# A two-block convolution network on one core: a partition shuffle moved from TensorE to transfers

## The reference

```python
x = x + L0(_gn(x), p1, p3, p4, p5, p6)
x = x + L1(_gn(x), conv_w, gamma, beta)
```

```python
t1 = einsum('nchw,he->ncew', x, p1)                      # e = 16
t3 = depthwise conv of t1, 9 x 9, weights p3
t4 = grouped conv of t3, 5 x 1, four channels a group, p4
t5 = einsum('ncew,ewf->ncf', t4, p5)                     # f = 384
t6 = depthwise conv of t5 over f, 3 taps, p6
out = einsum('ncf,nfp->ncp', t6, t2) / sqrt(384)         # t2: three row shifts of x
```

## Time and profile before

| | |
|---|---|
| median of 3 runs | 300.83 us |
| lowest and highest | 298.19 and 301.51 us |
| the profiled execution's own time | 300.65 us |
| its span in the profile | 298.9 us |
| TensorE busy, share of the span | 85% |
| VectorE | 77% |
| ScalarE | 62% |
| GpSimd | 47% |

### The profile page before, as it was taken

How to read it: one execution, slowest core, us unless ns; L and a number is a source line. 1 busy time by engine, 2 the same in 40 slices (tenths; PEclk the granted TensorE clock), 3 DMA queues, 4 the chain that set the end, 5 groups by cost and what they waited for, 6 DMA issues and landing times.

```text
span 298.9 us, 6443 instructions
## 1 busy us (share of the span) xinstructions
PE 253.4 (85%) x2558; PEld 193.1 (65%) x2558; DVE 230.4 (77%) x543; ACT 186.6 (62%) x262; POOL 140.0 (47%) x136
## 2 busy tenths in 40 slices
PE   8999979989798998999999999999999999850000
PEld 4444456555454877988899889988899886630000
DVE  1898974454456777688999999999999997786991
ACT  2799613325344534776778877877778877456990
POOL 4000000005033204787988889888988889640000
PEclk9999979999999999999999999999999999975555
DMA  7996122432200700000000000000000000001798
GB/s 220 411 409 260 41 86 83 141 130 83 72 4 3 279 4 0 0 0 2 0 2 2 0 3 0 0 2 0 1 2 0 0 1 2 1 0 50 315 403 355
DMA packets 8445, 25.18 MB, mean 84 GB/s; under 512 B 1248, under 2 KB 1376, under 8 KB 8416
## 3 DMA queue, kind: packets, MB, share of 16 engines
q1 hardware_dynamic: 7184, 20.32, 18.7%
q10 hardware_dynamic: 1232, 4.46, 3.9%
HBM read 16.39 MB, written 8.39 MB: 83 GB/s over the span
## 4 chain that ended last, share of the span: by engine, by line
PE 75%; DVE 10%; issue 5%; DMA 2%; POOL 2%; ACT 2%; DVEq 0%; POOLq 0%; ACTq 0%
PE low L232 10%; PE low L234 9%; PE low L233 9%; PE low L562 9%; PE low L586 8%; DVE x_sb L986 5%; PE high L621 5%; PE high L699 4%; PE high L232 4%; PE high L234 4%; PE high L233 4%; PE high L708 3%; DMA x_sb<-in_x 2%; PE high L601 2%; DVE t_sb L778 2%
## 5 line engine op out<-in xcount | busy, mean ns | idle before, releaser
L379 POOL TENSOR_TENSOR g_lo<-y_sb,g_hi 128x1024 fp32r<-128x1024 f32 x15 | 36.1, 2408 | 14.4 <-ACT y_sb L521 14.4
L355 POOL TENSOR_TENSOR g_lo<-y_sb,g_hi 128x1024 fp32r<-128x1024 f32 x15 | 35.9, 2390 | 13.6 <-ACT g_hi L478 13.6
L232 PE MATMUL low<-g_hi,t_hi 128*128 128x512 f32 x96 | 37.6, 391 | 1.3 <-DVE t_lo L886 0.7
L234 PE MATMUL low<-g_hi,t_lo 128*128 128x512 f32 x96 | 37.5, 391 | 0.0
L233 PE MATMUL low<-g_lo,t_hi 128*128 128x512 f32 x96 | 37.5, 390 | 0.0
L346 POOL TENSOR_TENSOR p_lo<-p_raw,p_hi 128x384 fp32r<-128x384 f32 x4 | 3.9, 1004 | 65.2 <-ACT p_hi L443 65.2
L519 ACT ACTIVATE g_hi<-x_sb,rs 128x1024 fp32r<-128x1024 f32 x15 | 19.9, 1329 | 18.7 <-POOL rs L364 18.7
L562 PE MATMUL low<-xa,p_blk 128*128 128x512 f32 x64 | 28.0, 595 | 0.2 <-DVE xa L770 0.2
L770 DVE STREAM_TRANSPOSE xa<-x_sb 128x512 f32<-128x512 f32 x32 | 19.9, 681 | 8.5 <-DMA x_sb<-in_x 8.2
L857 DVE TENSOR_TENSOR x_sb<-x_sb,low 128x512 f32<-128x512 f32 x32 | 21.7, 677 | 6.1 <-PE low L234 5.9
L232 PE MATMUL high<-p_hi,d_split 128*128 128x384 f32 x68 | 24.5, 360 | 0.0
(11 more groups left out here) (156 smaller groups left out, 664.4 us busy)
## 6 DMA issues: line engine op xcount, KB each, us to landing
out<-x_sb SPq DMA_DIRECT2D x6, 1024.0 KB, 4.9
x_sb<-in_x SPq DMA_DIRECT2D x11, 512.0 KB, 9.4
x_sb<-in_x ACTq DMA_DIRECT2D x8, 512.0 KB, 13.8
taps<-in_taps SPq DMA_DIRECT2D x6, 320.0 KB, 3.7
mix<-in_mix SPq DMA_DIRECT2D x6, 256.0 KB, 3.2
out<-x_sb SPq DMA_DIRECT2D x3, 512.0 KB, 2.8
p_raw<-in_p SPq DMA_DIRECT2D x1, 768.0 KB, 5.8
taps_third<-in_taps SPq DMA_DIRECT2D x2, 320.0 KB, 4.5
```

The source lines that it names most:

```text
L232: nc.tensor.matmul(ps, w[0], m[0], start=start, stop=False)
L234: return nc.tensor.matmul(ps, w[1], m[0], start=False, stop=stop)
L355: pool.tensor_tensor(g1_lo[:, W:W + HW], y_sb[:, n, :], g1_hi[:, W:W + HW].bitcast(F32), ALU.subtract).then_inc(s["g1_lo"], 1)
L379: pool.tensor_tensor(g2_lo[:, :], y_sb[:, n, :], g2_hi[:, :].bitcast(F32), ALU.subtract).then_inc(s["g2_lo"], 1)
```

## The change

For the steps 0 to 4 (`RS = 5`) the permutation by identity products goes. In its place sixteen transfers from `t4_sb` to a new tensor `d_st` (three slots) carry the same blocks: six from SP, ten from GpSimd. The steps 5 to 7 keep the identity products. The conversions of d follow two steps behind instead of one (`D_AT`): steps 4 and 5 both stand behind the t3 copy of step 6. The mix product of steps 1 to 5 waits for the copy of t4 instead of the rest of d; the copy of t4 of step r waits until the transfers of step r - 2 have read the slot.

`d_st` takes the space of images 9 to 11, so seven images instead of four are loaded again, now also behind the output products of two images. Image two has buffers of its own for g1 in the space of images 14 and 15, and its conversion waits for no product. In turn 1 VectorE takes the first half of the moments ahead of the second addition. The load of w moves ahead of the last wait for a mix product.

The core of the diff:

```diff
-RESIDENT = 12
-TR = 3
+RESIDENT = 9
+USED_FIRST = 12
+RS = 5
+D_AT = {2: (0,), 3: (1,), 4: (2,), 5: (3,), 6: (4, 5), 7: (6,)}
+BY_SP = 6
+TR, DR = 3, 3
...
+        d_st = put("d_st", [DR, CI, B, JC * NO])
...
+        cursor[0] = region_t - 2 * HW * 4
+        second_hi = put("second_hi", [HW], F32R)
+        second_lo = put("second_lo", [HW], F32R)
...
+        def shuffle(eng, r, some, done):
+
+            eng.wait_ge(s["t4_ev"], 2 * (r + 1))
+            if r >= DR:
+                eng.wait_ge(s["d_lo"], 2 * (r - DR + 1))
+            for jl, co in some:
+                eng.dma_start(d_st[32 * jl:32 * jl + 32, r % DR, co].rearrange("p b k -> p (b k)"),
+                              t4_sb[32 * co:32 * co + 32, r % 2, jl].rearrange("p b k -> p (b k)")
+                              ).then_inc(done[r % DR], 16)
+
+        def shuffled(eng, r):
+            for done, some in ((d_in, BY_SP), (d_in_pool, len(blocks) - BY_SP)):
+                eng.wait_ge(done[r % DR], 16 * some * (r // DR + 1))
...
                 load_taps(r)
+                if r == R - 1:
+                    sp.dma_start(w_raw[:, :, :], w_in).then_inc(s["w_raw"], 16)
                 sp.wait_ge(s["d_mm"], 2 * (r - TR + 1))
                 load_mix(r)
+                shuffle(sp, r - TR, blocks[:BY_SP], d_in)
...
+            for r in range(RS):
+                shuffled(sp, r)
             sp.wait_ge(s["d_mm"], 2 * R)
-            sp.wait_ge(s["perm"], R)
+            sp.wait_ge(s["perm"], R - RS)
+            sp.wait_ge(s["o_mm"], 2)
...
+            for r in range(RS - 1):
+                shuffle(pool, r, blocks[BY_SP:], d_in_pool)
             for jc in range(JC):
                 pool.wait_ge(s["p5_hi"], jc + 1)
...
+            shuffle(pool, RS - 1, blocks[BY_SP:], d_in_pool)
             pool.wait_ge(s["gst"], 1)
...
             def d_high(r):
-                act.wait_ge(s["perm"], r + 1)
+                if r < RS:
+                    shuffled(act, r)
+                else:
+                    act.wait_ge(s["perm"], r - RS + 1)
...
-                if r >= 1:
-                    d_high(r - 1)
+                for q in D_AT.get(r, ()):
+                    d_high(q)
...
-                if n >= 1:
+                if n >= 2:
                     act.wait_ge(s["o_mm"], n)
-                act.copy(g1_hi[:, W:W + HW], g1_f(n)).then_inc(s["g1_hi"], 1)
+                (hi, _), first = g1_parts(n)
+                act.copy(hi[:, first:first + HW], g1_f(n)).then_inc(s["g1_hi"], 1)
...
-                    if t == MID and r >= 2:
+                    if t == MID and r - 2 >= RS:
                         permute(r - 2)
...
-                if 1 <= r < R - 1:
+                if 1 <= r <= RS:
+                    pe.wait_ge(s["t4_ev"], 2 * r)
+                elif RS < r < R - 1:
                     pe.wait_ge(s["d_lo"], 2 * r)
...
-                    if r >= 2:
-                        dve.wait_ge(s["perm"], r - 1)
+                    if r - 2 >= RS:
+                        dve.wait_ge(s["perm"], r - 2 - RS + 1)
+                    elif r >= 2 and h == 0:
+                        shuffled(dve, r - 2)
...
-                d_low(r)
+                for q in D_AT.get(r + 1, ()) if r < R - 1 else (R - 1,):
+                    d_low(q)
...
-                if t == N:
+                if t in (1, N):
                     x1_half(t - 1, 0)
```

More of the change, by code:

```diff
@@ L145, in build @@
         cursor[0] = region_t - (N - RESIDENT) * HW * 4
+        d_st = put("d_st", [DR, CI, B, JC * NO])
         t4_sb = put("t4_sb", [2, JL, B, JC * NO])
+        assert cursor[0] >= region_t - (N - USED_FIRST) * HW * 4
         taps_third = put("taps_third", [TCOLS])
         mix_third = put("mix_third", [MCOLS])
+        assert cursor[0] <= region_t
+        cursor[0] = region_t - 2 * HW * 4
+        second_hi = put("second_hi", [HW], F32R)
+        second_lo = put("second_lo", [HW], F32R)
         assert cursor[0] <= region_t
@@ L200, in build @@
         x_in = [sem(f"s_x_in{n}") for n in range(N)]
+        d_in = [sem(f"s_d_in{k}") for k in range(DR)]
+        d_in_pool = [sem(f"s_d_in_pool{k}") for k in range(DR)]
         taps_sem = [sem(f"s_taps_in{k}") for k in range(TR)]
@@ L220, in g2_parts, with g1_parts @@
             return (g2_hi, g2_lo) if n < N - 1 else (last_hi, last_lo)
+        def g1_parts(n):
+            return ((second_hi, second_lo), 0) if n == 1 else ((g1_hi, g1_lo), W)
         def g1_f(n):
@@ L252, in d_columns @@
         def d_columns(r, h):
+            if r < RS:
+                return d_st[:, r % DR, 2 * h:2 * h + 2, :, :].rearrange("p c b (j n) -> p b j n c", j=JC)
             return ps_mix(r)[:, 2 * h:2 * h + 2, :].rearrange("p c (b j n) -> p b j n c", b=B, j=JC)
+        blocks = [(jl, co) for jl in range(JL) for co in range(CI)]
+        def shuffle(eng, r, some, done):
[9 more added lines that the diff above has]
+                eng.wait_ge(done[r % DR], 16 * some * (r // DR + 1))
         block = ctx.enter_context(nc.Block())
@@ L288, in _ @@
                          allow_slow_non_contiguous=True).then_inc(s["p6_in"], 16)
-            sp.wait_ge(s["x_used"], 2 * (N - RESIDENT))
+            sp.wait_ge(s["x_used"], 2 * (N - USED_FIRST))
             sp.wait_ge(s["t1_mm"], NO)
@@ L354, in g1_low @@
                 pool.wait_ge(s["g1_hi"], n + 1)
-                pool.tensor_tensor(g1_lo[:, W:W + HW], y_sb[:, n, :], g1_hi[:, W:W + HW].bitcast(F32),
+                (hi, lo), first = g1_parts(n)
+                pool.tensor_tensor(lo[:, first:first + HW], y_sb[:, n, :], hi[:, first:first + HW].bitcast(F32),
                                    ALU.subtract).then_inc(s["g1_lo"], 1)
@@ L662, in out_product @@
                 pe.wait_ge(s["g1_lo"], n + 1)
+                (hi, low_part), first = g1_parts(n)
                 for hh in range(2):
@@ L667, in out_product @@
                         i0, i1 = (1 if hh == 0 and k == 0 else 0), H // 2 - (1 if hh and k == 2 else 0)
-                        lo, to = (H // 2 * hh + k) * W, HALF * hh
+                        lo, to = (H // 2 * hh + k - 1) * W + first, HALF * hh
                         mm = split_product(ps_o[:, to + W * i0:to + W * i1], (t6_hi[:, k, :], t6_lo[:, k, :]),
-                                           (g1_hi[:, lo + W * i0:lo + W * i1], g1_lo[:, lo + W * i0:lo + W * i1]),
+                                           (hi[:, lo + W * i0:lo + W * i1], low_part[:, lo + W * i0:lo + W * i1]),
                                            k == 1, k == 2)
@@ L787, in d_low @@
                     ins.then_inc(s["d_lo"], 1)
-            halves = [(n, hh) for n in (*range(RESIDENT, N), *range(BY_ACT, RESIDENT)) for hh in range(2)]
+            halves = [(n, hh) for n in (*range(USED_FIRST, N), *range(BY_ACT, USED_FIRST)) for hh in range(2)]
             for n, hh in halves:
@@ L948, in _ @@
                     x1_add(t - 1, 1)
-                    if t < N:
+                    if 1 < t < N:
                         x1_half(t - 1, 0)
```

1 line of the change is left out of this document (removed).

## The result

| | us |
|---|---|
| before, median of 22 runs beside the changed kernel | 299.31 (297.36 to 301.85) |
| changed kernel, median of 22 runs | 303.81 (299.60 to 309.24) |
| ratio | 1.0087 [1.0057, 1.0116] |
| changed kernel again, another set, 4 runs | 304.47 (302.58 to 307.13) |
| ratio there | 1.0160 [1.0112, 1.0208] |

A ratio leaves out the runs that lie over 1.5% above the fastest of the same kernel, nine of the changed kernel's 22 here. By the ratios the change costs 0.9% in the one set and 1.6% in the other, about the 1% that can be told from none and above it; by the medians of all runs it costs 1.5% and 2.0%. I had forecast 1.4% less. The first profiled execution of the changed kernel, 309.24 us (span 307.5), is the longest of its 22 runs, so a second was profiled in the other set: 304.03 us (span 302.3). What follows is read in both, and the second is the one to go by.

A forecast was written before the change was run, and what follows sets the result against it. The prediction took TensorE's own work and the handovers to it as the bound of the convolution stage; 3.0 us there plus 1.0 us at image two off 300.65 gave 296.65, stated as 296.6 us, range 294.0 to 318.0.

The forecast's parts named there:

- 4.45: Convolution stage: us gained on TensorE by removing five permutations, 0.89 per round, taken as the most possible.
- a = 0.47: GpSimd's issue pitch, us per transfer, taken from SP's image loads; bounds 0.26 and 2.2.
- The first rival: GpSimd's issue bounds the convolution stage at a pitch of 0.66 or more: 308 us at 0.8, 318.0 at 1.0; chance 0.30.
- Image two: Start of the long stage: image two's output products start at 116.1 instead of 117.14, gain 1.0 us (0.6 to 1.3).
- the formula behind step three's t4: Time from step three's share on GpSimd to step four's landing: twenty issues, p5 subtraction 3.88, completion 2.0 us; landing at 83.1.
- three and four come to 67.8 and 74.05: Ends of the t4 copies of steps three and four, in us, with three and four permutations gone before them; earlier 70.50 and 77.61.
- traffic alone isn't their cause, and I count them as unchanged: Convolution stage: TensorE's unexplained idle pieces stay as before, 1.2 us either way for the range.
- The cover of 1.8 us: ScalarE's slack after step zero's conversion, done at 56.5, before the end of convolution three at 58.3; gone at pitch 0.65.
- my own sign of error: Convolution stage: forecast is wrong if ScalarE's conversions wait for transfers by over 4 us in each round.
- I leave it out of the sum: VectorE's rests contending with GpSimd's p5 subtraction in the convolution stage, delaying that subtraction once by 1.76 us; sum 1.8 us less.
- The third: Rival: instruction supply to TensorE bounds the convolution stage; only image two's 1.0 us is left, 299.6 us; chance 0.05.
- The second: Rival: TensorE's gain is given back before mix six, pitch 0.56 to 0.65 or slow landing; 299.9 us at 0.6; chance 0.11.

The follow-up runs named there:

- The stage without transfers: Changed kernel with each step's sixteen transfers replaced by one GpSimd memset: 291.34 us, ratio 0.9739 to the kernel before.
- Traffic alone: Kernel before with image two's own buffers, all eight permutations kept, sixteen unread transfers beside each of steps 0 to 4: 304.97 us.
- the unread kernel: Changed kernel with all its transfers, but conversions and rests of steps 0 to 4 read t4 itself: 295.72 us, ratio 0.9886 to the kernel before.

## Why the prediction was wrong

**Right: what is removed, and the round.** A round of 5.50 us was predicted, 5.37 is measured. The stage without transfers gains 6.3 us, so 4.45 was too low by nearly 2; I had called it "the most that the stage can give".

**Right: the number on which the forecast was to hang.** I chose a = 0.47, and 0.49 is measured. The estimate of 1.0 from the Trainium skill ("DMA: Bandwidth & Descriptors", "Latency and other measured facts") as a cost per transfer is refuted by these rows; as a delay of the first byte it is compatible with the 2.1 us median to landing. The first rival (a of 0.66 or more) falls with it, though its sign came true. The measured time lies inside the stated range only because this rival, which didn't happen, carried it to 318.0: that is luck. I hung the forecast on the wrong number.

**Right: image two.** 1.0 us was predicted, 1.08 is read.

**Right: the formula behind step three's t4.** 20a + 3.88 + 2.0 gives 15.7; in the second profile GpSimd begins that share at 73.14 and ScalarE is released at 89.52, 16.4 later; mix six then begins 4.42 later (4.3 predicted). What failed is its starting point, "three and four come to 67.8 and 74.05": step three's share began at 73.14, with the third convolution 0.9 us *earlier* than before. So TensorE was over 6 us behind by then. In between stand the pieces of 1.31 and 3.74 (5.05, where 1.65 stood before over the same rounds, of which 0.96 is in the earlier trace rows: 3.4 more), the wait of 1.19 for t3, and taps and mix at a low clock (0.4 and 1.2 more): 6.2 together.

**Wrong: "traffic alone isn't their cause, and I count them as unchanged".** I read that a 1.63 us piece stood where the DMA share was 0.02, and from "traffic isn't needed for a piece" went on to "traffic doesn't lengthen one". The small piece too ended 1.4 us after a transfer of instructions; it shows what a piece waits for, and not that traffic can't make the wait longer. Traffic alone measured +6.9 us beside the permutations and +4.8 without them, and priced at "nothing, with that cover" it was the term missed. It didn't turn the sign by itself: with all transfers made and not read the kernel is still 1.1% faster than before. With the late landings of the next step it did. The mean share of 0.29 could not have told, and the share of a slice doesn't either: it is 1.00 at 63 to 65 us here, and 0.97 in the kernel with unread transfers, in which TensorE was busy all of that time.

**Wrong: SP's pitch and the landing of a share.** "0.47 each", measured 0.7 to 0.9. "Step zero landed at 55.3": issues were over at 53.2 in the second profile, but ScalarE was released at 58.19, 5.0 us later and not 2.0, with step one's sixteen issued right behind. The cover of 1.8 us was gone, and as the prediction says of that case, the copy of t3 was late and then the next convolution, by 1.19 us. ScalarE waits 15.8 us in four such waits in the first profile, and my own sign of error, over 4 us a wait, is met in three of them; a granted clock below full was another such sign, 0.91 and 0.93. On TensorE the late landings show as 1.19, 0.93 and 2.09 us in the second profile. By the times, what hangs on them is 6 to 8 us, the longer pieces and the half clock included.

**Wrong by omission: "I leave it out of the sum".** The Trainium skill ("SBUF — State Buffer", "Who interferes with whom") says that a VectorE instruction with two SBUF inputs and a GpSimd one that reads SBUF exclude each other. In the first profile it happened ahead of mix six, with GpSimd's build of w and not with p5:

```profile
93.31 0.46 POOL L378 TENSOR_TENSOR w_f<-w_det 128x128 f32<-128x128 f32 x1
...
93.01 3.64 DVE L840 TENSOR_TENSOR d_split<-d_st,d_split 128x136 fp32r<-128x136 f32 x8 [2.90 <-ACT d_split L481]
```

3.64 instead of 1.77 is 1.87 us, the 1.76 that I had named. In the second profile the eight rests of step four took 1.81, so this meeting comes in one execution and not in another; how much of the changed kernel's scatter it makes is not shown. I had the loser wrong: here it is VectorE.

**The rivals.** The third, "the removed ones leave longer unexplained pieces", had the mechanism nearest to the truth and a chance of 0.05; I gave it no loss beyond the gain. The second, the gain given back before mix six, came true as well. Both together, with the transfers making the pieces longer, gave a result that none of the three priced. The 299.9 us that the second rival has at a = 0.6 is a slip: its formula gives 300.65 - 0.4 - 1.0 = 299.2.

**The account**, from medians and, for the landings, ratios: permutations off and image two's buffers, -7.2 to -7.7; traffic, +4.8; the landings and what rides on them, +6 to +8. The last is the difference between two measured kernels, so that the sum comes out near 304 is no test of it.

## What to carry to other kernels

Where TensorE runs hundreds of small matmuls and shows idle pieces with no semaphore behind them, don't price added transfers by bytes or by DMA share: try the traffic alone, unread, beside the old kernel, and look in the trace at when the instruction queue's transfers land. One wide transfer was free here and sixteen narrow ones a step cost more than the work that they replaced. A formula of queue times is only as good as its starting point: ask first what could make the producer late.

## What the hardware did that I had not expected

- Unread transfers hold up TensorE's matmuls, by 4.8 to 6.9 us for eighty transfers of 34 KB; five of 544 KB cost nothing beside 1035 matmuls and 2.4 to 2.8 us beside 1195 (the counts of the stretch). What is held up is the supply of instructions: every idle piece of 0.2 us or more with no semaphore behind it in this stage ends 1.1 to 1.7 us after a 16 KB transfer of the instruction queue.
- SP's issue of a transfer took 0.47 us for image loads and 0.6 to 0.9 for 32 or 128 rows from SBUF to SBUF.
- VectorE and GpSimd seem to exclude each other by whole instructions. In the kernel without transfers four p5 subtractions met the rests:

```profile
66.85 4.12 POOL L386 TENSOR_TENSOR p_lo<-p_raw,p_hi 128x384 fp32r<-128x384 f32 x4
...
66.49 5.06 DVE L837 TENSOR_TENSOR d_split<-d_st,d_split 128x136 fp32r<-128x136 f32 x8 [0.67 <-ACT d_split L478]
```

GpSimd took 4.12 instead of 3.88, VectorE 5.06 instead of 1.77: some of its 0.29 us subtractions lasted up to 1.11 us, about one of GpSimd's (1.06). In the unread kernel one lasted 2.23 and the eight 3.71.
